# Moving a PSUM copy and two matmul groups in a pipelined spectral mixer: the down product's copy one chunk later, the second mix chunk among the transposes

## The reference

```python
x = _L0_conv_ref(x, raw_kernel, bias)          # lat * x + bias + x
t = _to_tokens(x)
t = t + _L1_attn_ref(_ln_t(t), ...)
t = t + _L1_ffn_ref(_ln_t(t), W1, b1, W2, b2)

# _L1_attn_ref
h = relu(bn(x @ w1.T))                         # 192 features
X = fft(h, axis=tokens)
xr = relu(X.real * rd - X.imag * idg + rb)
xi = relu(X.imag * rd + X.real * idg + ib)
y = ifft(xr + 1j * xi).real
o = bn(y @ w2.T)                               # back to 96
# _L1_ffn_ref: q_mul rounds to 5 exponent and 2 mantissa bits, q_acc to 5 and 10
h = relu(q_acc(q_acc(q_mul(x) @ q_mul(W1).T) + q_mul(b1)))   # 384 hidden
y = q_acc(q_acc(q_mul(h) @ q_mul(W2).T) + q_mul(b2))
```

## Time and profile before

| what | value |
|---|---|
| median of the runs | 6206.72 us |
| profiled execution, its own time | 6218.28 us |
| its span in the trace | 6216.1 us |
| busy: PE, DVE, ACT, POOL | 5297.6, 4527.8, 3248.1, 1951.5 us |
| share of the span | 85%, 73%, 52%, 31% |
| granted PE clock, mean over the span | 0.951 |

### The profile page before, as it was taken

The page is one execution under the profiler, slowest core; times in us unless marked ns, Lnnn a source line. Parts: engine busy times, 40 slices in busy tenths (PEclk is TensorE's granted clock), DMA queues, the critical chain, the costliest instruction groups (busy, mean ns, idle before and its releaser), DMA issues. The chain is left out here.

```text
span 6216.1 us, 136648 instructions
## 1 busy us (share of the span) xinstructions
PE 5297.6 (85%) x44298; PEld 4566.4 (73%) x44298; DVE 4527.8 (73%) x12660; ACT 3248.1 (52%) x6469; POOL 1951.5 (31%) x1924
## 2 busy tenths in 40 slices
PE   8999996488888888888888888888888888888887
PEld 8889996377777777777777777777777777777775
DVE  4555664457777777777777777777777777777776
ACT  0000000256666666666666666666666666666664
POOL 0000000123333333434333343334333333333343
PEclk9999998689999999999999999999999999999995
DMA  6665655355555555555555555555555555555552
GB/s 223 180 188 171 193 171 161 85 137 140 139 137 137 141 137 136 141 142 139 139 139 138 140 139 141 142 141 139 140 140 141 139 140 142 139 136 138 139 139 55
DMA packets 681435, 892.28 MB, mean 144 GB/s; under 512 B 240785, under 2 KB 629130, under 8 KB 659530
## 3 DMA queue, kind: packets, MB, share of 16 engines
q1 hardware_dynamic: 610124, 800.99, 50.7%
q10 hardware_dynamic: 71174, 89.35, 4.7%
HBM read 505.60 MB, written 384.61 MB: 143 GB/s over the span
## 5 line engine op out<-in xcount | busy, mean ns | idle before, releaser
L664 POOL TENSOR_TENSOR spec<-spec,gc 96x400 f32<-96x400 f32 (+1 forms) x512 | 488.7, 955 | 2473.3 <-DVE spec L864 2473.3
L1007 PEld LDWEIGHTS ps<-fb,acol 100*96 100x96 f32 x7936 | 778.8, 170 | 316.0 <-DVE gv L868 233.7
L1007 PE MATMUL ps<-fb,acol 100*96 100x100 f32 x7936 | 815.4, 257 | 124.2 <-DVE gv L868 116.2
L675 POOL TENSOR_TENSOR z<-z,b2q 121x384 f16<-121x384 f16 (+1 forms) x448 | 397.4, 887 | 1560.0 <-ACT z L779 1560.0
L989 PE MATMUL ps<-hid,fa 121*128 121x384 f32 (+1 forms) x1792 | 708.6, 477 | 187.5 <-DVE arow L854 106.7
L707 ACT ACTIVATE hid<-ps,rstd 121x192 f32<-121x192 f32 x1600 | 602.7, 432 | 482.8 <-PE ps L978 482.6
L1034 PE MATMUL ps<-w2t,spec 97*100 97x96 f32 x3968 | 718.2, 264 | 19.1 <-DVE spec L875 19.1
L259 DVE SCALAR_TENSOR_TENSOR xout<-cps,xin 114x351 f32<-114x351 f32 (+3 forms) x512 | 402.4, 786 | 443.0 <-PE cps L286 443.0
L1036 PE MATMUL ps<-w2t,spec 96*100 96x96 f32 x3968 | 702.3, 260 | 0.0
L667 POOL TENSOR_SCALAR gv<-gv 96x400 f32<-96x400 f32 (+1 forms) x512 | 663.9, 1297 | 106.4 <-DVE gv L868 106.3
L854 DVE COPY arow<-ps 128x384 f32<-128x384 f32 (+1 forms) x896 | 454.3, 507 | 323.9 <-PE ps L989 293.7
(11 more groups left out here) (101 smaller groups left out, 11296.9 us busy)
## 6 DMA issues: line engine op xcount, KB each, us to landing
a_d<-arow SPq DMA_DIRECT2D x256, 384.0 KB, 3.6
acol<-a_d SPq DMA_DIRECT2D x64, 1200.0 KB
grow<-g_d SPq DMA_DIRECT2D x128, 600.0 KB, 7.4
tok<-x_d SPq DMA_DIRECT2D x64, 1134.4 KB
t_res<-x_d SPq DMA_DIRECT2D x64, 1134.4 KB
acol<-a_d SPq DMA_DIRECT2D x64, 1125.0 KB
a_d<-arow SPq DMA_DIRECT2D x192, 288.0 KB, 5.1
xin<-in_x SPq DMA_DIRECT2D x256, 211.5 KB, 5.7
```

The source lines that it names most:

```text
L1007: last = nc.tensor.matmul(ps[0:HH, 2 - 2 * (t % 2) + n // 4, 128 * (n % 4):128 * (n % 4) + Q], acol[:, p0 + n, hf * HH:(hf + 1) * HH], fb[ ...
```

## The change

`narrow` moves one chunk later in ACT's list: `narrow(c-2)` stands at the end of iteration c, where `narrow(c-1)` stood. In PE's list the call of `down` moves from the end of the loop body to its start, and its index from c-1 to c-2. `mix(0)` moves to between the second and third turn, and `mix(1)` moves out of the loop to between the fourth and fifth turn. Each `mix(c)` now waits for the gate tiles `s_ready` and `d_ready` that hold its pairs (2, 4, 4, 6, 6, 8, 8 tiles); `mix(0)` still waits for `v_ready` of all 8 tiles.

```diff
+EARLY_MIX = 2
...
-                for c in range(NC + 1):
+                for c in range(NC + 2):
                     if second and c < NC:
                         out_w2(c)
                     if third and c < NC:
                         wide(c)
-                    if second and c:
+                    if second and 1 <= c <= NC:
                         out_inverse(c - 1)
-                    if third and c:
-                        narrow(c - 1)
+                    if third and c >= 2:
+                        narrow(c - 2)
...
                 def mix(c):
                     b = i - 1
+                    tiles = 2 * ((MIXED[c + 1] - 1) // KC) + 2
                     if c == 0:
                         pe.wait_ge(v_ready, b * TILES + TILES)
-                        pe.wait_ge(s_ready, b * TILES + TILES)
-                        pe.wait_ge(d_ready, b * TILES + TILES)
+                    pe.wait_ge(s_ready, b * TILES + tiles)
+                    pe.wait_ge(d_ready, b * TILES + tiles)
...
-                        if second and c == 4:
-                            mix(0)
+                        if second and c in (2, 4):
+                            mix(c // 2 - 1)
...
                 for c in range(NC + LAG):
-                    if second and c < NC and not (third and c == 0):
+                    if third and 2 <= c < NC + 2:
+                        down(c - 2)
+                    if second and c < NC and not (third and c < EARLY_MIX):
                         mix(c)
                     if third and c < NC:
                         up(c)
...
-                    if third and 1 <= c <= NC:
-                        down(c - 1)
```

## The result

The changed kernel takes 6703.63 us (median of four runs, 6697.9 to 6709.6) against 6208.38 us: slower by a factor of 1.0788, 95% interval 1.0754 to 1.0822. The forecast of 6336 us, range 6270 to 6400, had the direction and not the size: +495 us where it said +129.

The account below looks back on a forecast made before the run. PE, busy 86%, was taken to bound the kernel. A part: 75.8 + 0.7 + 2.3, with the clock 79.4 us, +2.0 against the mean; times 62 +124, +5 for the last parts: 6336 us, range 6270 to 6400.

Parts of the forecast that it names:

- Part 1: `mix(1)` moved into the turns: a part 0.7 us longer up to turn 4, nothing back at `up(1)`; bounds 0 and 1.8.
- Part 2: ACT's z copy (`narrow`) one chunk later: `down(1)` to `down(4)` start later, 2.3 us a part; bounds 0.5 and 3.5.
- Part 3: PE's clock: falls in about half of the parts around `up(0)`, few at the old place; 0.6 us a part, ends 0 and 1.6.
- at least as often as today: Rival on PE's clock: falls cost 1.6 us a part, +3.0 us a part in all, 6398 us; chance 0.15.
- The two that claimed hidden or useful waits: Rivals: `narrow` ends before `down`, 6207 to 6255 us, chance 0.06; freeing `wide` on ACT shortens chunks, 6126 us, chance 0.05.
- That `down` gets no more distance from `up`: In the loop, PE's order does not change, so the later `narrow` gives `down` no extra distance; no size of its own.

Follow-up runs that it names:

- the filled run: The changed kernel plus eight matmuls of constants, result not read, in front of `up(1)`; z copy still one chunk later: 6378.8 us, ratio 1.0259 against the kernel before.

## Why the prediction was wrong

**Part 1, mix(1) into the turns: right.** It said +0.7 us a part at full clock and nothing back at `up(1)`. `up(0)` came 0.61 us later, and parts without a fall last 76.4 us with the gap filled and the z copy at its old place, +0.6. `up(1)` waited 1.56 us. The two chunks pull apart: `mix(0)` won 0.5 us, `mix(1)` cost 1.1.

**Part 2, the z copy: right, the sum 0.4 too large.** The chain of copies was forecast at 3.19 and 2.66 us and measured at 3.18 and 2.65. `down(1)` to `down(5)` wait for the z copy, as it named them. A part grew by 1.9 us, not 2.3, as the way from `up(6)` to `down(6)`, which is DVE's chain, took 5.54 us instead of 5.95; the sum had carried it over unchanged, although Part 3 of the prediction let the wait ahead of `down(6)` shrink to 1.2 us (measured 1.04).

**Part 3, the clock: the step that failed.** "I take 0.6 us a part; the ends are 0 and 1.6." The changed part lasts 85.3 us, and 75.8 + 0.6 + 1.9 = 78.3, which the filled run shows as it is, leaves 7.0 us for the clock. The place was named rightly, the cluster around `up(0)`, and the falls at the old place, ahead of which `down(6)` waits, went as forecast. Two things were wrong. The fall comes in every part, not in half of them, and it lasts 20.5 us, not the 3.4 us of the earlier trace rows. I took the length of a fall from stretches that lay in transposes, `mix`, row and column products, and put its price at 1.4 us wherever it lands. At the new place the fall lasts six times as long, although PE is busy for 18.90 of the 20.5 us. Both ends of the term were therefore drawn from the wrong place. With the term at 7.0 the sum is 85.3 - 77.4 = 7.9 us a part, 62 x 7.9 = 490, and 5 for the tail (the last two parts grew from 76.9 to 82.4 us): +495 us.

The right place was in the trace of the kernel before. Its last part with both stages enters the same loop at half clock, and the clock is back only at 6114.8, where the first `inverse_rows` ends:

```profile
6084.10:6114.80 30.70, 28.89 (x156) 24.94 (x157) 5.84 (x13) 11.71 (x16) 3.87 (x5) 0.50 0.05 13
```

Even the line of the earlier trace rows that priced the bare wait says it: the three `up` matmuls in it last 1.37 us, at full clock 0.78.

Of the rivals, the clock falling "at least as often as today" was the nearest, but its price per fall was the same wrong one. The two that claimed hidden or useful waits failed as the rows said: `wide` was never late. That `down` gets no more distance from `up` was the most valuable sentence of the prediction: giving it that distance is worth 335 us.

What stays open: why the clock fell in each part, at the same point behind its first turn, while in other runs the parts alternate; why the same open wait brings 20.5 us at half clock in one part and none in the next; and what ends a low stretch. Whether the first `inverse_rows` ends it in the changed kernel was read off the timeline, not tested.

## What to carry to other kernels

Check where a moved call really lands: here the new index and the new place in the loop cancelled on one engine and not on the other, and a copy meant to run further behind ended up in front of its consumer. Before moving work out of a gap, ask what that work covered: `mix(1)` hid a 1.5 us wait, and taking it out cost 1.1 us in time and 7 us in clock. A price for a clock fall holds only for the place where it was measured; look in the trace for a fall that the same instructions follow, its rare parts at the end included, and keep the upper end of the term wide.

## What the runs showed of the hardware

- PE can stay at half clock while it is fully busy: 20.40 of 20.40 us busy at 0.50, in the run with ten narrow matmuls. It can also come back after 6.80 of 6.80 us, in the run with both chunks early and `down` later.
- In the changed kernel the fall followed a stretch in which PE was busy for 1.26 of 3.40 us, with no single wait over 1.56 us.
- With four fp32 matmuls of 400 columns behind `down(0)` the clock was back after 6.8 us; with ten of 96 columns, about the same time on PE, it was not.
- Eight matmuls without use made a kernel faster by 325 us, because they lay in a wait.
